# A feed-forward's first projection by seven quarter products per pair of blocks, with the weight quarters streamed from DRAM

## What is computed

```
xn = layernorm(x)
h  = square(relu(xn @ W_fc.T))          # 512 -> 2048
y  = h @ W_proj.T                       # 2048 -> 512
count = spikes that y causes in 5 steps of a leaky neuron
s  = layernorm((softmax(q k^T) + bias) v) * gamma + beta
out = x + s * silu(count / 5)
```

## Time and profile before

| What | us |
|---|---|
| median of three executions | 3533.66 |
| the profiled execution (span) | 3528.6 |
| PE busy in it | 3421.4 (97%) |
| ACT busy | 2624.2 (74%) |
| DVE busy | 2506.6 (71%) |
| POOL busy | 1720.5 (49%) |

### The profile page before, as it was taken

The page is one execution under the profiler, slowest core; times in us unless marked ns, Lnnn a source line. Parts: engine busy times, 40 slices in busy tenths (PEclk is TensorE's granted clock), DMA queues, the critical chain, the costliest instruction groups (busy, mean ns, idle before and its releaser), DMA issues.

```text
span 3528.6 us, 55344 instructions
## 1 busy us (share of the span) xinstructions
PE 3421.4 (97%) x19961; PEld 1441.3 (41%) x19964; DVE 2506.6 (71%) x4051; ACT 2624.2 (74%) x3898; POOL 1720.5 (49%) x998
## 2 busy tenths in 40 slices
PE   7999999999999999999999999999999999999996
PEld 3444444444444444433433433433433433433431
DVE  5555555555555555777888888888888888888887
ACT  6433333333333335999999999999999999999997
POOL 0012222111111123899666666666666666666672
PEclk9999999999999999999999999999999999999999
DMA  5122322333222222222322322322322322322322
GB/s 186 57 80 80 104 79 80 101 96 103 80 79 79 81 83 86 83 67 72 121 88 84 95 87 83 96 87 84 96 85 83 98 85 82 100 85 82 100 61 84
DMA packets 238752, 312.35 MB, mean 89 GB/s; under 512 B 96624, under 2 KB 132208, under 8 KB 238480
## 3 DMA queue, kind: packets, MB, share of 16 engines
q1 hardware_dynamic: 238480, 308.82, 28.2%
HBM read 174.65 MB, written 76.61 MB: 71 GB/s over the span
## 4 chain that ended last, share of the span: by engine, by line
ACT 33%; PE 11%; issue 10%; DVE 4%; SPq 1%; DMA 1%; ACTq 0%; POOL 0%; DVEq 0%; POOLq 0%
ACT recurrence_or_probs L1457 17%; ACT s_sb L1464 16%; PE misc L1331 3%; PE acc L1406 3%; PE s_ps L1386 3%; PE s_ps L1372 2%; DVE s_sb L1533 2%; DMA xT<-xnT 1%; SPq L322 1%; DVE gate_or_tokens L1662 0%; PE misc L1313 0%; DVE outT L1553 0%; DVE x_or_queries L1570 0%; DVE gate_or_tokens L1665 0%; PE s_ps L1331 0%
## 5 line engine op out<-in xcount | busy, mean ns | idle before, releaser
L1739 POOL TENSOR_TENSOR recurrence_or_probs<-recurrence_or_probs,toep 128x512 f32<-128x512 f32 (+1 forms) x375 | 1288.5, 3457 | 366.5 <-ACT recurrence_or_probs L1457 366.2
L1533 DVE TENSOR_SCALAR_CACHE_REDUCE s_sb<-s_ps 128x1024 f32<-128x1024 f32 x998 | 1213.7, 1220 | 353.8 <-PE s_ps L1372 325.7
L1464 ACT ACTIVATE s_sb<-s_sb,nmax 128x1024 f32<-128x1024 f32 x998 | 1167.0, 1169 | 9.8 <-DVE s_sb L1533 9.5
L1457 ACT ACTIVATE recurrence_or_probs<-s_ps 128x1024 f32<-128x1024 f32 x1024 | 1060.1, 1036 | 7.7 <-PE s_ps L1386 7.5
L559 PE MATMUL ps_fc<-xnT_part,w_fc 128*128 128x512 f16 x3072 | 707.2, 380 | 4.5 <-DVE w_fc L817 4.5
L574 PE MATMUL ps_y<-w_pr,hid_part 128*128 128x512 f16 x3072 | 706.2, 380 | 3.6 <-issue 2.6
L740 ACT ACTIVATE relu<-ps_fc 128x512 f32<-128x512 f32 x256 | 152.7, 597 | 626.9 <-PE ps_fc L559 626.9
L130 POOL TENSOR_TENSOR recurrence_or_probs<-gate_or_tokens,beta_row 128x512 f32<-128x512 f32 x60 | 89.9, 1499 | 1035.3 <-DVE gate_or_tokens L185 1031.7
L929 DVE TENSOR_TENSOR hid<-relu 128x512 f32<-128x512 f32 x256 | 210.3, 822 | 510.9 <-ACT relu L740 510.9
L1406 PE MATMUL acc<-recurrence_or_probs,val 128*32 128x512 f32 x4096 | 545.2, 604 | 2.2 <-DVE recurrence_or_probs L1649 1.5
L559 PEld LDWEIGHTS ps_fc<-xnT_part,w_fc 128*128 128x128 f16 x3072 | 300.6, 98 | 369.3 <-issue 7.8
(11 more groups left out here) (180 smaller groups left out, 2685.1 us busy)
## 6 DMA issues: line engine op xcount, KB each, us to landing
toep<-table_rows SPq DMA_DIRECT2D x32, 2048.0 KB, 8.3
x_or_queries<-x_or_queries SPq DMA_DIRECT2D x384, 64.0 KB, 2.0
x_or_queries<-in_x SPq DMA_DIRECT2D x16, 1024.0 KB, 10.4
xnT<-xnT_part SPq DMA_DIRECT2D x32, 512.0 KB, 8.5
x_or_gate<-in_x SPq DMA_DIRECT2D x16, 1024.0 KB, 9.2
base<-x_or_gate SPq DMA_DIRECT2D x16, 1024.0 KB, 6.8
xT<-xnT SPq DMA_DIRECT2D x32, 512.0 KB, 9.7
result<-gate_or_tokens SPq DMA_DIRECT2D x64, 256.0 KB, 2.0
```

Source lines behind the costliest of these rows:

```text
L1457: nc.scalar.activation(prob[:, k % PROBS, 2 * second:2 * second + 2, :].rearrange("p j n -> p (j n)"), s_ps[:, item_buffer(pair_item(m)), ...
L1464: nc.scalar.activation(s_sb[:, i % 4, :], s_sb[:, i % 4, :], ACT.Exp, bias=nmax[:, par, j, st:st + 1], scale=-1.0, accum_out=den[:, par, j ...
L1533: nc.vector.tensor_scalar(s_sb[:, i % 4, :], s_ps[:, item_buffer(tile_item(n)), :], -1.0, None, ALU.mult, ALU.min, accum_out=nmax[:, par, ...
L1739: nc.gpsimd.tensor_tensor(tile, tile, toep[:, par, :, at:at + width], ALU.add).then_inc(biased, 1)
```

## The change

Blocks go in pairs. A pair's 256x512 part of W_fc is taken as a 2x2 matrix of quarters (128 features by 256 inputs), the chunk's xn as a 2x2 matrix of quarters (256 inputs by 256 tokens), and their product is made by seven quarter products instead of eight (Winograd's form of Strassen's scheme), from sums and differences of quarters:

- POOL makes four sums of weight quarters per pair once (`sum_quarters`) and, for each chunk, four sums of token quarters (`make_turns`); the latter are split into hi and lo like xn (`turned_hi` on ACT, `turned_lo` on DVE) and transposed by DMA into a new tile `xnS`.
- PE makes per pair seven `product`s of 6 matmuls of 256 columns in place of 24 of 512 columns, with the `proj` tiles of earlier blocks set between them. Three PSUM sums (`sum_a`, `sum_b`, `sum_c`) are used; ACT copies intermediate states of `sum_a` out (`snapshot`, `take_sum`) and DVE adds them (`combine`) to get the four quarters of the result. Relu and square are one DVE instruction.
- The weights in this form (917 KB per pair) no longer fit SBUF. They are written to DRAM once (`store_quarters`) and each pair is loaded again from there into a ring of three (`load_quarters`, issued from ACT).
- The spike steps, the sigmoid and the gate go token tile by token tile.
- x of chunk c+2 is loaded after the transposes of chunk c+1, since the sums of token quarters lie where x lay; the hi and lo parts of those sums lie where xn lay, so `normalise` waits for the transposes of the chunk before (semaphore `xs_turned`).

The attention stage is as it was. The core of the diff:

```diff
 def turn(c, par):
-    wait(sp, fc_done, (c - 1) * FB)
+    wait(sp, multiplied, (c - 1) * PAIRS * PRODUCTS)
     wait(sp, xt_stored, (c - 1) * 32)
     for part, done in ((0, xn_hi), (1, xn_lo)):
         for t in range(4):
             sp.wait_ge(done, (c - 1) * 4 + t + 1)
             for k in range(EB):
                 sp.dma_start(xnT[:, par, part, k, t * P:(t + 1) * P], xn_part[:, part, t, k * P:(k + 1) * P],
                              transpose=True).then_inc(xt_turned, 16)
+    if c == 1:
+        sp.wait_ge(fc_lo, 8)
+    for part, done in ((0, turn_hi), (1, turn_lo)):
+        for j in range(4):
+            sp.wait_ge(done, (c - 1) * 4 + j + 1)
+            for t in range(2):
+                for k in range(2):
+                    sp.dma_start(xnS[par][:, part, j, k, t * P:(t + 1) * P], turn_part[:, part, j, t, k * P:(k + 1) * P],
+                                 transpose=True).then_inc(xs_turned, 16)
...
-                if ahead:
-                    load_x(c + 1)
...
+                if c < NC - 1:
+                    turn(c + 1, 1 - par)
+                if c < NC - 2:
+                    load_x(c + 2)
...
+def make_turns(c):
+    b11, b21, b12, b22 = (xn[:, 2 * s:2 * s + 2, k * HALF:(k + 1) * HALF] for s in range(2) for k in range(2))
+    pool.wait_ge(xn_ready, c * 4 + 4)
+    nc.gpsimd.tensor_tensor(turns[:, TURN_3], b22, b12, ALU.subtract).then_inc(turns_made, 1)
...
+def product(n, i):
...
+    elif i == 2:
...
+        elif p == 0:
+            pe.wait_ge(xs_turned, c * TURNED)
+        pe.wait_ge(snapped, n * 4 + 1)
+    elif i == 3:
+        pe.wait_ge(combined, n * 3 + 1)
...
+    for k in range(2):
+        for a, b in TERMS:
...
+            last = nc.tensor.matmul(bank, w["fc"][:, n % RINGW, i, a, k, :], moving,
+                                    start=(m == 0 and i in (0, 1, 3)), stop=(m == 5), skip_group_check=True)
...
+def load_quarters(n):
...
+    act.wait_ge(multiplied, (n - RINGW + 1) * PRODUCTS)
+    nc.scalar.dma_start(w["fc"][:, s].rearrange("p i a k n -> p (i a k n)"), d["fc_made"][source]).then_inc(fc_loaded[s], 16)
...
 def normalise(c, t):
...
-    wait(dve, xn_lo, (c - 1) * 4)
-    wait(dve, xn_hi, (c - 1) * 4)
+        wait(dve, xs_turned, (c - 1) * TURNED)
...
+def combine(n, i):
+    out, bank, m = ((u11, sum_b, 0), (u22, sum_c, 2), (u21, sum_c, 1))[i]
+    dve.wait_ge(multiplied, n * PRODUCTS + (2, 4, 7)[i])
+    dve.wait_ge(snapped, n * 4 + (1, 3, 2)[i])
+    nc.vector.tensor_tensor(out, bank, snap[:, m, :], ALU.add).then_inc(combined, 1)
...
+# DVE, step of pair n = 8c + p (late: 1 in chunk 0, else 0)
+    square(2 * n - 1)
+    first_max(n - 1, 3)
+    if ahead and p == 0 + late:
+        statistics(c + 1, 0)
...
+    combine(n, 0)
...
+    if ahead and p == 1 + late:
+        refine(c + 1)
+        normalise(c + 1, 0)
...
+# PE, step of pair n
+    a, b = 2 * n - 3, 2 * n - 2
+    product(n, 0)
+    proj(a, 0)
+    product(n, 1)
+    proj(a, 1)
+    first_tile(n, 0)
+    product(n, 2)
+    proj(a, 2)
+    product(n, 3)
...
+    proj(a, 3)
...
+    product(n, 4)
...
+    proj(b, 0)
+    proj(b, 1)
+    product(n, 5)
+    proj(b, 2)
...
+    product(n, 6)
+    proj(b, 3)
```

## The result

The changed kernel takes 3994.18 us (median of four runs, 3991.72 to 3995.54), the kernel before 3532.72 beside it. The ratio is 1.1314 with a 95% interval of 1.1300 to 1.1328: 13% slower. (One of the four runs of the kernel before was disturbed, at 3928.31; the ratio leaves it out.) The prediction was 3980 us, in a range of 3885 to 4110.

What follows compares the result with a forecast made beforehand. SP's 64 transposes per chunk, in a closed loop with load, normalisation and first pairs, were to bound it: fourteen turns of 113.4 us put the feed-forward's end 448 us later, giving 3980 us, range 3885 to 4110.

Steps and rivals of the forecast that it cites:

- PE's price: On PE, a pair costs 9.77 us against 10.36, saving 76 us over 128 pairs.
- The transposes: In SP's queue, 64 transposes per chunk at 1.30 us take 83.1 us, plus 1.2 until the last has landed.
- The rest of the turn: From PE's restart to the next chunk's first transpose: 7.7 + 5.9 + 9.8 + 3.4 + 2.3 us.
- until the fourth product (load of x, statistics, combine): At a chunk's restart, PE's fourth product waits for x, DVE's statistics and combine: 7.7 us (5.7 to 10.4).
- rest of the pair, with the low clock: On PE, 4 products and 5 tiles take 5.9 us, plus 2.3 for the lower clock after standing still.
- next pair: The second pair of the turn, in which x is normalised, takes 9.8 us.
- until the first transpose: In the third pair, product, snapshot, weight-load issue, hidden copy and ACT's first hi part take 3.4 us.
- The ends: First transpose of chunk 0 at 66 us, chunk 1 turns at 150, chunk 15 at 1738, feed-forward ends at 1838.
- Hidden transposes: Rival: SP's transposes stay hidden and PE remains the bound, if one costs under 0.86 us: 3468 us; chance 0.03.
- The open loop: Rival: SP is late, but normalisation gets ahead of the transposes; a chunk is SP's own 92 us: 3680; chance 0.05.
- The weight stream as the main cause: Rival: weight loads delay transposes, each starting only when the one before has landed: about 5020 us; chance 0.03.
- DVE as the next bound: Were PE's idle time gone, DVE would be the closest to binding, with some 59 us of 78 per chunk.

Runs made afterwards that it cites:

- 48 transposes: Changed kernel with one DMA per token tile for the new transposes of the sums alone, 48 per chunk in place of 64: 3686.89 us.
- the late statistics: Changed kernel with DVE's four statistics of the next chunk's x moved behind the pair's second combine: 3928.86 us.
- DVE's order mended: Changed kernel with 24 transposes per chunk, turned sums' lo parts behind the third combine, attention weights' lo parts spread in three pairs: 3475.61 us.
- the wide kernel: Changed kernel with one DMA transposing all feature blocks of a token tile, 24 transposes per chunk in place of 64: 3489.66 us.

## Why the prediction was right, step by step

**PE's price.** A pair was put at 9.77 us; the rows have 9.76 (854.02 to 863.78). With the transposes out of the way chunks come to 78.4 us against the 78.2 of eight pairs, and the time falls by 53 us of the 76 named.

**The transposes** were put at 83.1 us and 1.2 to the landing, 84.3; from the first one's start to PE's restart it is 87.62 us (752.32 to 839.94). The pace was 1.30 us in the sum and is (86.43 - 1.23) / 63 = 1.35 in this chunk, inside the upper bound of 1.37. This term was too small by 3.3 us in this turn, and by 2.6 in the mean of 14 (86.9). Of these some 1.6 go with the weight stream, as the run with a seventh of it shows (85.7 against 84.1 us for 64 transposes); the rest is not accounted for. To cost the stream at nothing was the one step that was wrong in kind, and it is worth 22 us of 3994.

**The rest of the turn** was put at 29.1 us and is 26.36 in this turn (26.9 in the mean):

| Term | Predicted | Measured | Rows |
|---|---|---|---|
| until the fourth product (load of x, statistics, combine) | 7.7 | 6.68 | 839.94 to 846.62 |
| rest of the pair, with the low clock | 5.9 + 2.3 | 7.40 | 846.62 to 854.02 |
| next pair | 9.8 | 9.76 | 854.02 to 863.78 |
| until the first transpose | 3.4 | 2.52 | 863.78 to 866.30 |

The load of x landed 6.7 us after its issue (838.86 to 845.54), where 7.7 had been taken, and so 0.9 us earlier in the turn. The issue of the weight load on ACT, for which there was no row, takes 0.33 us (at 854.88) and not 0.9. The clock did fall at each restart, and cost a little less than the 2.3 us assumed: the rest of the pair is 1.5 us over its 5.9 in this turn, 2.0 in the mean. So the turn of 113.4 us, measured 113.8, came out so close by luck, from two errors that cancel: in the mean the transposes were 2.6 us too short and the rest 2.2 too long. The mechanism is shown apart from that: by the four products of one turn in rows, by 48 transposes (93.5 us), by the late statistics (109.1) and by the kernel before with doubled transposes.

**The ends.** Chunk 0's first transpose stood at 65.09 us (66). Chunk 1 turned at 154.57 (150): its 64 transposes took 88.3 us, the longest of the 15 sets. They run beside the loads of the start, but no run tested whether that is why. Chunk 15 turned at 1745.21 (1738), and the feed-forward ended at 1850.8 (1838): PE waited 4.7 us for score tiles where 3 had been allowed, and 4 more us of the last chunk are not accounted for. The attention is as it was. The bounds of the range, 3885 and 4110, were counted from 3976, the profiled execution; for the median both should stand some 5 us higher, which changes nothing.

**The rivals.** Hidden transposes were to give 3468 us; where fewer instructions hide them, 3489.7 comes out, and 3475.6 with DVE's order mended, so that number was sound and its condition, under 0.86 us per 128x128 block, was what failed at one block per instruction. The open loop, 3680, fell by the 48 transposes, for which it would have given PE's own pace. The weight stream as the main cause, 5020, fell with the seventh of it. DVE as the next bound was right in place: of the wide kernel's waits in the middle of the feed-forward all are for DVE, at 63.9 of 80 us busy, where the prediction had 59 of 78.

## What to carry to other kernels

Count the instructions of a queue, not their bytes: a DMA transpose held its issuer here as long for one 128x128 block as for four (1.23 and 1.27 us), so give it as wide a tile as its source allows before adding more of them. An in-order queue with no busy row, such as SP's, can become the bound without any line of the busy times showing it; add up its issues per chunk, and then look for a wait by which the next chunk's issues hang on this chunk's last one, for such a loop pays every latency in it once per turn (here some 27 us on top of 87). When PE waits for a result of DVE, look up which instruction the semaphore belongs to and what stands ahead of it in DVE's row order; moving the neighbour of the culprit made it worse.

## What the hardware showed beyond the expected

- A transpose of 128x512 fp16 (131 KB) holds SP for 1.27 us and lands 3.0 us after its issue by the median, one of 128x128 (33 KB) for 1.23 and 2.4 (2.9 in the changed kernel). That is 104 GB/s while it is issued, against 27. The Trainium skill, VectorE: DVE Perf Modes, section The three transpose paths, gives 1309 ns for a 128x128 block by DMA; the pace of one block per instruction here, 1.35 us, agrees with it, but with four blocks in an instruction the same time buys four. The 350 to 400 GB/s of Advanced Engine Details and Errata, section X-Bar Transpose (TRN2), in the Trainium skill, were reached by the transposes in no run.
- DVE's spike step (L171) took 0.68 us while POOL stood idle (it did until 566.44) and 1.75 beside instructions on POOL, in the wide kernel:

```profile
564.98 0.68 DVE L171 SCALAR_TENSOR_TENSOR recurrence_or_probs<-recurrence_or_probs 128x512 f32<-128x512 f32 x1
...
568.07 1.60 POOL L125 TENSOR_TENSOR x_or_gate<-x_or_gate,recurrence_or_probs 128x512 f32<-128x512 f32 x1
568.47 1.75 DVE L171 SCALAR_TENSOR_TENSOR recurrence_or_probs<-recurrence_or_probs 128x512 f32<-128x512 f32 x1
```

The Trainium skill, GPSIMD Engine Reference, section 1. Specifications, says that GpSimd shares its SBUF interfaces with VectorE and contends with instructions there that read two SBUF inputs; L171 is one, and the rows agree. No run here moved the work of POOL to test it.
- In the first 6 us of each restart (after 17 to 37 us of idle time) the granted clock was 0.50 to 0.75 of the full 2.4 GHz, at 12 of 15 restarts 0.50, the lower level of 1.2 GHz; in the wide kernels, where PE hardly stands, it was 1.00 in the stretches shown.
